# Keys and queries kept unsplit in memory, half of the weight pieces quantised in the first part, statistics a half ahead

## What is computed

```python
x = x + attn(layernorm(x))
x = x + ffn(layernorm(x))
# attn: c_q = x @ W_DQ; Qc = c_q @ W_UQ; Qr = rope(c_q @ W_QR)
#       c_kv = x @ W_DKV; Kc = c_kv @ W_UK; Kr = rope(x @ W_KR), one for all 16 heads; V = c_kv @ W_UV
#       softmax(clip([Qc Qr] [Kc Kr]^T, -80, 80) / sqrt(48), causal) @ V @ W_O
# ffn:  fp4_linear(silu(fp4_linear(x, w_gate)) * fp4_linear(x, w_up), w_down)
# fp4_linear quantises both operands in blocks of 16 to the 8 magnitudes of FP4 and multiplies
```

## Time and profile before

| | us |
|---|---|
| median of 3 runs (3183.49 to 3189.47) | 3185.83 |
| the profiled execution | 3188.37 |
| its span, first to last instruction | 3186.5 |
| first part: first projection to last | 22 to 377 |
| attention: first score to last product | 416 to 1407 |
| feed-forward | from 1411 |
| PE busy over the span | 96% |
| DVE busy | 82% |
| ACT busy | 38% |
| POOL busy | 21% |

### The profile page before, as it was taken

One profiled execution on the slowest core, in us unless ns is written; L12 is line 12 of the kernel. 1 busy time (PEld: TensorE's weight loads), 2 busy tenths in 40 slices (PEclk: granted clock), 3 DMA queues, 4 the chain that ended last, 5 costly groups with the idle time before them and its releaser, 6 DMA issues.

```text
span 3186.5 us, 65504 instructions
## 1 busy us (share of the span) xinstructions
PE 3045.8 (96%) x23492; PEld 2232.9 (70%) x23492; DVE 2602.1 (82%) x4432; ACT 1222.7 (38%) x1833; POOL 657.6 (21%) x632
## 2 busy tenths in 40 slices
PE   7999779999999999988999999999999999999999
PEld 6777534444444444447888888888888888888887
DVE  6777558888888888887888888888888888888886
ACT  3544346666666666662222222222222222222221
POOL 2334300000000000002233333233223223222332
PEclk9999889999999999999999999999999999999999
DMA  6999965665656656551000000000000000000000
GB/s 228 333 341 337 317 161 164 168 175 155 187 168 172 174 156 189 163 173 56 30 30 30 30 30 24 29 28 28 30 30 30 30 30 30 30 30 30 30 24 14
DMA packets 234506, 351.37 MB, mean 110 GB/s; under 512 B 17616, under 2 KB 117840, under 8 KB 234448
## 3 DMA queue, kind: packets, MB, share of 16 engines
q1 hardware_dynamic: 234448, 350.59, 36.0%
HBM read 205.55 MB, written 144.97 MB: 110 GB/s over the span
## 4 chain that ended last, share of the span: by engine, by line
PE 54%; DVE 1%; ACT 0%; issue 0%; POOL 0%; DVEq 0%
PE p_ring L1548 19%; PE p_ring L1576 15%; PE ps_od L1548 11%; PE ps_od L1528 5%; PE p_ring L1566 2%; PE p_ring L1556 1%; DVE sb_wg_lo L1444 0%; PE ps_od L1576 0%; PE p_ring L1528 0%; PE p_ring L1591 0%; DVE sb_fp_tmp L102 0%; DVE sb_wd_lo L1444 0%; DVE sb_h_amax L88 0%; DVE sb_stage L1415 0%; DVE sb_ht_lo L1433 0%
## 5 line engine op out<-in xcount | busy, mean ns | idle before, releaser
L780 ACT ACTIVATE sb_probs<-scores 128x1024 f32<-128x1024 f32 (+3 forms) x768 | 586.2, 813 | 395.5 <-PE scores L969 384.6
L839 DVE TENSOR_SCALAR sb_probs<-sb_probs 128x2048 f32<-128x2048 f32 (+3 forms) x320 | 288.3, 901 | 91.3 <-ACT sb_probs L780 88.3
L984 PE MATMUL ps_od<-sb_probs,sb_v 128*32 128x512 f32 (+3 forms) x3072 | 328.1, 499 | 0.7 <-DVE sb_probs L831 0.7
L1246 POOL TENSOR_TENSOR sb_stage<-sb_stage,sb_h_inv 128x512 f32<-128x512 f32 (+1 forms) x192 | 210.4, 1096 | 543.3 <-DVE sb_h_inv L94 543.3
L969 PEld LDWEIGHTS scores<-sb_q_hi,sb_k_hi 32*128 32x128 f32 x1536 | 73.7, 182 | 345.4 <-ACT sb_probs L780 284.7
L1548 PE MATMUL p_ring<-sb_wg_hi,sb_xq_hi 128*128 128x512 f32 (+1 forms) x1024 | 295.3, 369 | 0.3 <-DVE sb_wd_lo L1444 0.3
L1548 PE MATMUL p_ring<-sb_wg_lo,sb_xq_hi 128*128 128x512 f32 (+1 forms) x1024 | 290.9, 365 | 0.0
L1548 PE MATMUL p_ring<-sb_wg_hi,sb_xq_lo 128*128 128x512 f32 (+1 forms) x1024 | 289.9, 364 | 0.0
L1576 PE MATMUL p_ring<-sb_wd_hi,sb_ht_hi 128*128 128x512 f32 x693 | 275.9, 398 | 0.0
L831 DVE SCALAR_TENSOR_TENSOR sb_probs<-sb_probs,sb_bound 128x512 f32<-128x512 f32 x256 | 174.7, 682 | 121.6 <-ACT sb_probs L780 121.6
L1576 PE MATMUL p_ring<-sb_wd_hi,sb_ht_lo 128*128 128x512 f32 x693 | 270.2, 390 | 0.0
(11 more groups left out here) (180 smaller groups left out, 6653.2 us busy)
## 6 DMA issues: line engine op xcount, KB each, us to landing
kq<-sb_kq_out SPq DMA_DIRECT2D x64, 1024.0 KB, 8.1
sb_xin<-in_L_attn_x_dram SPq DMA_DIRECT2D x32, 512.0 KB, 5.9
rq<-sb_r_out SPq DMA_DIRECT2D x32, 512.0 KB, 6.8
v<-sb_v_out SPq DMA_DIRECT2D x64, 256.0 KB, 6.0
sb_k_hi<-kq SPq DMA_DIRECT2D x32, 512.0 KB
sb_q_hi<-kq SPq DMA_DIRECT2D x32, 512.0 KB
sb_k_lo<-kq SPq DMA_DIRECT2D x32, 512.0 KB
sb_q_lo<-kq SPq DMA_DIRECT2D x32, 512.0 KB
```

The costliest lines, as they stand in the source:

```text
L780: act.activation(probs[:, k % PROBS, 2 * pair:2 * pair + 2, off:BANK], scores[(2 * k + pair) % RING2][:, :, off:BANK], ACT.Exp, scale=SCAL ...
L839: i = dve.tensor_scalar(pr, pr, P_MAX, P_MIN, ALU.min, ALU.max)
L984: mm = pe.matmul(ps_o[rows, off:BANK], v_sb[s][:, j, rows], probs[:, k % PROBS, i, off:BANK], start=(j == 0), stop=last)
L1246: pool.tensor_tensor(x, x, spread(h_inv[:, a // QB:b // QB], (b - a) // QB), ALU.mult).then_inc(h_y, 1)
```

## The change

In the first part keys and queries are stored once, unsplit: ACT copies K and Q out of PSUM and that alone frees the buffer, DVE's subtraction (L442) is gone, and K and Q are 2 stores per block, not 4. The columns of `W_QR` are sorted by pair member, so that R is one unit of 6 matmuls where R0 and R1 had 12: a block has 78 matmuls of 512 columns. The table of cosines and sines has four planes (2 MB) in place of two. DVE's products for R are two of 128 x 1024, and POOL's addition and subtraction and ACT's rounding are one each of 128 x 1024; rq is stored by 4 DMAs of half the size. C is two units, C0 (keys and values first) and C1, of one bank each. The statistics of block n+2 are taken by DVE behind R of block n; POOL's power for them stands between its addition and its subtraction for R. Behind X1 (KR in the last block) DVE quantises one weight piece with ten operations in a row; SP loads the next piece behind the stores of K and Q and stores the finished one at the block's end. These are pieces 0 to 15.

In attention the remaining 16 pieces are quantised one per two groups: scales in the first, rounding in the second. K and Q of a group are loaded unsplit (2 DMAs of 512 KB, not 4) into one buffer, `kq_raw`; ACT rounds them behind the exponentials at k = 1 and 2 of the group before (128 x 1024 each), DVE subtracts at k = 3 and 9, and PE waits for both before the group's first score. The division of the first half is moved: `turn` to k = 4, `invert` and `turn_back` to k = 10, `normalise` to k = 11, ahead of the `turn` of the second half. PE gets 20 small matmuls at the head of the part (`WARM_UP`).

The diff, cut to its core:

```diff
+UNITS1 = ["C0", "C1", "KR", "X0", "X1", "K0", "K1", "Q0", "Q1", "R", "V0", "V1"]
...
-HI1 = ["C", "X0", "X1", "K0", "K1", "Q0", "Q1", "V0", "V1"]
+HI1 = ["C0", "C1", "X0", "X1"]
+FREED_BY_ACT = ["K0", "K1", "Q0", "Q1", "V0", "V1"]
+FREED_BY_DVE = ["C0", "C1", "KR", "X0", "X1", "R"]
...
+        def freed(eng, n, name):
+
+            if name in FREED_BY_ACT:
+                eng.wait_ge(act_free, (n + 1) * len(FREED_BY_ACT) + (FREED_BY_ACT.index(name) + 1))
+            else:
+                eng.wait_ge(dve_free, (n + 1) * len(FREED_BY_DVE) + (FREED_BY_DVE.index(name) + 1))
...
                 for k, name in enumerate(("K1", "Q1")):
-                    sp.wait_ge(ps_free, unit(n, units.index(name)) + RING1 + 1)
-                    for s in range(2):
-                        sp.dma_start(kq_v[k, s, b, :, :, cols], kq_out[:, half, k, s]).then_inc(stored[half], 16)
-                sp.wait_ge(rope_lo, n * 3 + 3 + 3)
+                    freed(sp, n, name)
+                    sp.dma_start(kq_v[k, b, :, :, cols], kq_out[:, half, k]).then_inc(stored[half], 16)
+                if not last:
+
+                    sp.wait_ge(piece_ready, n + 1)
+                    sp.dma_start(piece_in[:], t["w_all"][n + 1]).then_inc(piece_loaded, 16)
+                sp.wait_ge(rope_lo, n * 2 + 2 + 2)
                 for s in range(2):
-                    sp.dma_start(rq_v[s, b, :, :, cols], r_out[:, half, s]).then_inc(stored[half], 16)
-                sp.wait_ge(ps_free, unit(n, units.index("V1")) + RING1 + 1)
+                    for c in range(2):
+                        sp.dma_start(rq_v[s, c, b, :, :, cols], r_out[:, half, s, c]).then_inc(stored[half], 16)
+                freed(sp, n, "V1")
                 for j in range(4):
                     sp.dma_start(v_v[b, half * 4 + j],
                                  v_out[:, half, j].rearrange("p (g d) -> p g d", g=GROUPS)).then_inc(stored[half], 16)
+                sp.wait_ge(piece_done, n + 1)
+                sp.dma_start(t["wq_all"][n], piece_y[:]).then_inc(piece_stored, 16)
...
-                units = units_of(last)
-                if not last:
-                    inverse_deviation(n + 1)
...
+                    (freed_last if last else freed)(pool, n, name)
+                    pool.tensor_tensor(a, a, b_, ALU.add).then_inc(rope_sum, 1)
+                    if name == "R" and not is_last(b):
+                        inverse_deviation(n + 2)
+
+                    pool.wait_ge(rope_hi, n * 2 + k + 1)
+                    pool.tensor_tensor(lo, a, hi, ALU.subtract).then_inc(rope_lo, 1)
...
-                        act.copy(kq_out[:, half, k, 0, 2 * m:2 * m + 2, :].bitcast(F32R), ps[:]).then_inc(act_hi, 1)
+                        act.copy(kq_out[:, half, k, 2 * m:2 * m + 2, :], ps[:]).then_inc(act_free, 1)
...
+                        act.wait_ge(rope_sum, n * 2 + 2)
+                        act.copy(r_out[:, half, 0].bitcast(F32R), turned[:, 0]).then_inc(rope_hi, 1)
             blocks(act, body)
...
+            row_stats(1)
...
+                    if name[0] == "C":
+                        k = int(name[1])
+                        dve.wait_ge(act_hi, hi_count)
+                        dve.tensor_tensor(c_lo[:, k], ps[:, 0], c_hi[:, k].bitcast(F32),
+                                          ALU.subtract).then_inc(dve_free, 1)
+                        if k == 1 and not last:
+                            normalise(n + 1)
...
+
+                        dve.wait_ge(rope_lo, n * 2 + 2)
+                        dve.tensor_tensor(turned[:, 0], ps[:, 0, :].unsqueeze(1).to_broadcast([P, 2, BANK]),
+                                          rope[:, 1:3, pos], ALU.mult)
+                        dve.tensor_tensor(turned[:, 1], ps[:, 1, :].unsqueeze(1).to_broadcast([P, 2, BANK]),
+                                          rope[:, 0:2, pos], ALU.mult).then_inc(dve_free, 1)
+                        if not is_last(b):
+                            row_stats(n + 2)
+                    elif name[0] == "X":
...
+                    if name == ("KR" if last else "X1"):
+
+                        dve.wait_ge(piece_loaded, n * 16 + 16)
+                        fp4_scales(dve, piece_in[:], piece_amax[:], piece_scale[:], piece_inv[:], piece_scaled,
+                                   n * SCALES_STEPS)
+                        own(dve, piece_scaled, n * SCALES_STEPS + SCALES_STEPS)
+                        dve.wait_ge(piece_stored, n * 16 + 16)
+                        y = blocks_of(piece_y[:])
+                        dve.tensor_tensor(y, blocks_of(piece_in[:]), spread(piece_inv[:], WP // QB),
+                                          ALU.mult).then_inc(piece_ready, 1)
+                        own(dve, piece_ready, n + 1)
+                        dve.tensor_scalar(piece_big[:], piece_y[:], MAGIC, None, ALU.mult).then_inc(piece_magic, 1)
+                        own(dve, piece_magic, n + 1)
+                        fp4_round(dve, piece_y[:], piece_big[:], piece_tmp[:], piece_rounded, n * ROUND_STEPS)
+                        own(dve, piece_rounded, n * ROUND_STEPS + ROUND_STEPS)
+                        dve.tensor_tensor(y, y, spread(piece_scale[:], WP // QB), ALU.mult).then_inc(piece_done, 1)
+
+            dve.wait_ge(s_rope, 16)
+            blocks(dve, body)
...
+                    ps = ring[slot(units, name)]
+
+                    if place >= RING1:
+                        before = units[place - RING1]
+                        (freed_last if last and before in FREED_BY_DVE else freed)(pe, n, before)
+                    else:
+                        freed(pe, n - 1, UNITS1[place - RING1])
...
+WARM_UP = 20
...
+            def load_raw(it2, s):
+
+                g = it2 * 2 + s
+                sp.wait_ge(raw_split, g * 2 + 2)
+                for k in range(2):
+                    sp.dma_start(kq_raw[:, k], t["kq"][k, bass.ds(g * NI, NI)].rearrange("i p t -> (i p) t")
+                                 ).then_inc(raw_loaded, 16)
...
                 g = it2 * 2 + s
-                heads = bass.ds(g * NI, NI)
-                get(k_hi[s][:], t["kq"][0, 0, heads].rearrange("i p t -> (i p) t"))
-                get(q_hi[s][:], t["kq"][1, 0, heads].rearrange("i p t -> (i p) t"))
-                get(k_lo[s][:], t["kq"][0, 1, heads].rearrange("i p t -> (i p) t"))
-                get(q_lo[s][:], t["kq"][1, 1, heads].rearrange("i p t -> (i p) t"))
...
             def body(it2, s, first, last):
                 if not first:
-                    before = (it2, 0) if s == 1 else (it2 - 1, 1)
-                    store_piece(*before)
                     if not last:
...
                         load(*following(it2, s))
-                    store(*before, 1)
+                    store(*preceding(it2, s), 1)
+                if s == 0:
+                    if not (isinstance(it2, int) and it2 == G2 - 1):
+
+                        sp.wait_ge(w_y, it2 + 1)
+                        load_piece(it2 + 1)
+                else:
+                    store_piece(it2)
+                if not (isinstance(it2, int) and it2 == G2 - 1):
+                    load_raw(it2 + 1, s)
                 if last:
...
+            def round_raw(it2, s, k):
+
+                act.wait_ge(raw_loaded, it2 * 64 + (s * 32 + 32))
+                act.copy((k_hi, q_hi)[k][s][:], kq_raw[:, k]).then_inc(raw_rounded, 1)
+
...
+                    if k in (1, 2) and not last:
+                        round_raw(*following(it2, s), k - 1)
+                    if k == 6 and s == 0:
+                        act.wait_ge(w_y, it2 + 1)
+                        act.mul(w_big[:], w_sb[:], MAGIC).then_inc(w_magic, 1)
...
+            def rest_of_raw(it2, s, k):
+
+                dve.wait_ge(raw_rounded, it2 * 4 + (s * 2 + k + 1))
+                dve.tensor_tensor((k_lo, q_lo)[k][s][:], kq_raw[:, k], (k_hi, q_hi)[k][s][:].bitcast(F32),
+                                  ALU.subtract).then_inc(raw_split, 1)
+
...
                     elif k == 3:
+                        if not last:
+                            rest_of_raw(*following(it2, s), 0)
+                        if s == 0:
+                            own(dve, w_scaled, scaled + 3)
+                            dve.tensor_scalar(w_inv[:], w_inv[:], TIES, None, ALU.mult).then_inc(w_scaled, 1)
+                    elif k == 4:
                         turn(it2, s, 0)
-                        own(dve, w_scaled, scaled + 3)
-                        dve.tensor_scalar(w_inv[:], w_inv[:], TIES, None, ALU.mult).then_inc(w_scaled, 1)
-                    elif k == 4:
-                        invert(it2, s, 0)
-                        own(dve, w_scaled, scaled + 4)
-                        dve.tensor_tensor(w, w, spread(w_inv[:], WP // QB), ALU.mult).then_inc(w_y, 1)
+                        if s == 0:
+                            own(dve, w_scaled, scaled + 4)
+                            dve.wait_ge(w_stored, it2 * 16 + 16)
```

(22 more changed lines are left out.)

268 lines of the change are left out of this document (134 added, 134 removed).

## The result

The changed kernel takes 3198.64 us (median of 7 runs, 3196.74 to 3200.83), the kernel before 3188.62 in the same comparison (7 runs): a ratio of 1.0036, 95% interval 1.0025 to 1.0046. It is 10 us slower, where I had forecast some 24 us less (3162, against the 3185.83 known then); and the first part's last matmul starts at 380.3 us, past the 360 that I had named as a sign of being wrong.

| stretch | before, us | after, us | difference |
|---|---|---|---|
| to the last projection (start of it) | 376.26 | 380.31 | +4.1 |
| from there to the first score | 39.96 | 45.72 | +5.8 |
| first score to the feed-forward's first matmul | 994.5 | 996.9 | +2.4 |
| from there to the end | 1775.8 | 1773.3 | -2.5 |

A forecast was written before the change was run, and what follows sets the result against it. PE was taken as the bound, busy 346.4 of 355 us in the first part and 940 of 990 in attention; -22.4 - 3 - 4 + 6 - 1 = -24.4 gave 3164.0 us profiled, 3162 us median, range 3145 to 3180.

The forecast's parts named there:

- PE's shorter row: First part, PE: six fewer matmuls of 0.233 us save 1.40 us per block, times 16: -22.4 us, the sure term.
- Behind it the piece ends at H + 19.2: First part, DVE: the piece, placed behind the X subtraction, ends 19.2 us after the block's head H.
- I count 0: First part, the rest: ACT's copies, SP's stores, DMA traffic and the larger cosine table together cost 0 us.
- Rival D: First part: a closed loop through rq, stores, x loads and statistics makes the kernel slower, 3211 us; chance 0.07.
- My 19.5 us: First part: length of the closed loop from power through stores and x loads to statistics, put under the block period.
- Rival C: First part: POOL's overlap with DVE takes the slack, block period 21.2 us, not 20.4; 3174 us, chance 0.20.
- My price of half a microsecond per microsecond of overlap: First part: each microsecond of POOL working beside DVE costs DVE about half of one.
- The gap: Between first part and attention: draining stays, loads shrink by 1 MB; -4 us, between 0 and -8.
- Attention: In attention, `normalise` ahead of the second half's `turn` costs 0.2 us of a group's path: +6 us.
- The end: Last piece stored one group sooner, W_O asked for some us later, feed-forward untouched: -1 us, within 2.
- Rival E: Attention: two DVE subtractions between clips cost PE 0.4 us each, +25 us; 3187 us, no change; chance 0.06.
- The warm-up matmuls: Head of attention: the 20 matmuls run long before the last load lands, leave the clock as today, count 0.

The follow-up runs named there:

- experiment 8: On top of experiment 5, POOL's subtraction for R waits until the normalisation is through, and V is stored ahead of rq: 3149.22 us.
- experiment 1: Changed kernel with SP storing the finished piece right behind the load of the next one, ahead of rq and V: 3169.61 us.
- experiment 5: On top of experiment 1, ACT rounds kr behind the copy of K0, not of K1: 3161.41 us.
- experiment 3: Changed kernel without the piece's ten DVE operations in the first part; pieces 0 to 15 pass unquantised, still loaded and stored: 3150.70 us.
- experiment 9: Experiment 8 plus, in attention, second half's turn ahead of first half's normalise and W_O asked for ahead of the last piece's store: 3147.06 us.
- experiment 10: On top of experiment 5, the 20 warm-up matmuls left out (WARM_UP = 0): 3276.14 us, ratio 1.0281 to the kernel before.

## Why the prediction was wrong

**PE's shorter row.** -22.4 us was right in size: in experiment 8 a block is 2.20 us shorter than before. 1.40 of it are the six matmuls; nearly all the rest is the wait, which costs 0.72 us by the matmuls' start times (the transposes begin 0.95 us after the last start before them, not 0.23), where its row says 0.54. The condition that I put beside it, that no other engine's row becomes longer than 20.4 us, is what failed.

**The failing step** is the one on DVE in the first part: "Behind it the piece ends at H + 19.2". In the changed kernel it ends at H + 24.1. I laid its ten operations end to end behind the X subtraction and never asked what they wait for. L477 waits for the store of the piece before, 2.65 us in each block and 7.0 in the last. Of the 37 us between my forecast and the result, 29 are this wait, by experiment 1: the last projection stands 23 us later (1.6 us a block) and the gap is 7 us longer. The other 8 are POOL's subtraction for kr over L477 (experiment 5). With it, "I count 0" for SP's row failed: I counted the issues and the bytes (DMA at 0.73, forecast 0.78), not who waits for the last of them.

**Rival D** had the mechanism, with its power, POOL's subtraction, rq and V, and gave slower; I closed it at the wrong place. I let it end at the load of x, and no statistics wait for x in a trace shown, past the start-up: they are a half earlier in name only, since behind R of block n is the head of block n+1, where they were taken before. But it was close. In the changed kernel x is asked for 4.9 us ahead of the block's head, where it was 9.7, and lands 1.3 us ahead of the statistics, where it was 5.0:

```profile
197.52 1.27 SPq L236 DMA_DIRECT2D sb_xin<-in_L_attn_x_dram  x2
```

The loop that sets the pace ends one DMA earlier, at the piece's store. My 19.5 us lacked R's products and the piece's operations, which stand inside the loop. Its chance was 0.07, and its 3211 us were closer than my 3162.

**Rival C, contention,** was right as a mechanism and hidden behind the loop: 8 us from kr's subtraction over L477 and up to 12 from R's over the normalisation. My price of half a microsecond per microsecond of overlap was too low; experiment 1 shows 1.05 / 1.20 and 1.03 / 1.29, so 0.8 to 0.9. The earlier trace rows would have given it: L102 overlaps POOL there for 0.89 us, not for its whole time, and loses 0.74. The rule of the Trainium skill (GPSIMD Engine Reference, § 8 Key points) names L477, which reads two SBUF operands, and the trace agrees. The normalising operation reads one, so by that rule it would have to run in a two-port mode, which no row shows or rules out. The section gives no size. The sum of 3162 us is what experiment 5 measures (3161.4), with 0.35 us ahead of the transposes as I had taken. That is partly luck: the contention was larger than my price, the period 20.55 us and not 20.4, and attention cost less than its +6.

**The gap:** -4 forecast, +5.8 measured, 7 of it the wait of the last block. The loads gave 2 us, not 3: the first scores wait for V's load, which lands 15.6 us after its issue in both kernels, and not for K and Q.

**Attention:** +6 forecast, +2.4 measured up to the feed-forward's first matmul. The wait for `turn` is longer by 0.45 us at each group's change, yet PE makes up nearly all of it; 2 us come from W_O asked for late, which I had seen and priced within -1 of "The end". The 2.5 us of the feed-forward are no gain that can be told from nothing: its code is the same in all these kernels, and from its first matmul to the end the profiled executions take from 1773.2 us (experiment 3) to 1778.3 (experiment 9). Rival E, a cost of the subtractions on DVE, didn't show: the groups grew by 0.05 us.

**The warm-up matmuls** "count 0": true of the clock, which is 0.50 in the first 4 us of scores and 0.67 in the next 10, near the lower level of 1.2 GHz at first, as before. But they are not nothing: without them the kernel of experiment 5 loses 115 us (experiment 10).
